# Expert results added into one residual row per token by accumulating indirect DMA, in place of one stored row per token and expert

## The chip, the cores and the metric

The kernel runs on one core of one Trainium2 chip. The metric is the device time of one execution in microseconds (us); three executions of the kernel before took 964.06, 964.85 and 967.42 us, median 964.85. A difference below about 0.3% of it can't be told from no change.

## The reference

Two transformer-like layers over x of 8 batches x 512 tokens x 128 features, each with a mixture of experts:

```
x = layernorm(x + L0_attn(x))        # windowed softmax attention, 16 heads, with its own residual
x = layernorm(x + L0_ffn(x))         # 16 experts of 128 -> 512 -> 128 (gelu), 4 chosen per token
x = layernorm(x + L1_attn(x))        # linear attention with decay, in chunks
x = layernorm(x + L1_ffn(x))         # 8 experts of 128 -> 512 -> 128 (silu gate), 2 chosen per token

L0_ffn:  w = softmax(top-4 logits);  fused = sum_k w[k] * expert[topi[k]](x)
L1_ffn:  w = softmax(top-2 logits);  out   = sum_k w[k] * expert[topi[k]](x) * 12**-0.5
```

The change concerns the two weighted sums over a token's experts, and the addition of x and the layernorm behind each.

## The kernel before

The five engines run programs written out by hand, tied by semaphores; each engine takes its instructions in the order of its program. There are four long stages and a last one.

1. **Attention of layer 0**, batch by batch. Behind it each batch's rows x1 (the output of the first layernorm) are kept in `xres`, the router picks 4 experts per token, and GpSimd scatters each row 4 times into `xs[0]` in DRAM, in which every expert has a region of its own (`scatter`, L651). A row of `xs` holds the row's high and low bf16 halves and one number: the row of `yt` for the result.
2. **Expert tiles of layer 0.** A table made by `tile_table` (L896) lists tiles of 256 rows, each of one expert, expert by expert; it is walked in groups of `RING` = 4 tiles, with two hidden tiles computed ahead. For a tile, SP loads the rows by a transposing DMA (`xt`, L499) and their numbers (`to_now`, L503), TensorE makes the hidden layer (L1715 to L1717) and the output (L1726, L1736), ScalarE does the gelu (L1359) and copies the output from PSUM to `ysb` (`take_out`, L1341), VectorE splits the hidden layer in two bf16 parts (L944, L945), and GpSimd (`store_tiles`, L707) writes `ysb` to `yt` by two indirect DMAs of 128 rows of 512 bytes (L714). Rows of a tile behind the expert's last token have a number out of bounds and are dropped. `yt` has one row for every (token, choice), so no two DMAs touch the same row and none waits for another; ScalarE alone waits for the landing of the tile four before (the ring slot of `ysb`).
3. **Linear attention of layer 1**, `linear_body`, batch by batch, with the sum of layer 0 ahead of it: SP loads the 4 result rows of each token (1 MB per batch, L548, with L558 for the first batch), ScalarE multiplies them by their weights `wres` (`scale_results`, L1388), VectorE adds them and x1 (`pair_up` L971, `add_up` L976; the first batch is done by VectorE alone, L1205), then takes the statistics (`y_stats`) and applies them (`x2_apply`). The other work of a body is the attention, the routing of layer 1 and the scatter to `xs[1]`.
4. **Expert tiles of layer 1**, as stage 2 with three matrices per expert.
5. **The last stage**, for each batch: SP loads the 2 result rows per token (512 KB), VectorE sums with weights (`final_sums`, L1043, 8 operations) and takes the statistics, GpSimd makes the scale and shift (`final_scales`, L697), ScalarE applies them (L1472), SP stores the output (L578). `mv2`, `rstd2`, `minus_mean` and `shift` have one buffer each, `yf` and `ow` two.

The part of `store_tiles` that matters:

```
for u in range(RING):
    pool.wait_ge(to_loaded[n][u], 16 * g + 16)
    pool.wait_ge(y_done[n], RING * g + u + 1)
    for s in range(S2):   # S2 = 2
        pool.indirect_dma_start(out=yt[n][:, :], out_offset=...(to_now[:, u, s:s + 1], 0), in_=ysb[:, u, s, :], ...)
```

Of the kernel before, what the change touches and what calls it, by code (L numbers as in the profile page):

```python
# [52 lines left out]
XW = 2 * D + 2  # L53
# [9 lines left out]
DVE_STEPS_1 = 18  # L63
# [56 lines left out]
def program(nc, x_in, w_all, wq_s, wk_s, wv_t, wo_t, gamma, beta, keys_t, rw_t, rb, b1, b2,  # L120
            w_write, w_read_t, decay, log_alpha, wr, const, const_b, out):
    ctx = ExitStack()
    with ctx:
# [8 lines left out]
        def sem(name):  # L132
# [44 lines left out]
        wres = sb("wres", [P, NT, K0])  # L177
# [32 lines left out]
        table = sb("table", [1, TILES + 1], I32)  # L210

# [45 lines left out]
        to_now = sb("to_now", [P, RING, S2], U32)  # L257
# [9 lines left out]
        gat0 = sb("gat0", [P, 2, T, K0, D])  # L267
# [14 lines left out]
        gat1 = sb("gat1", [P, FIN, T, K1, D])  # L282
        yf = sb("yf", [P, 2, T, D])
        minus_mean = sb("minus_mean", [P, T])
        shift = sb("shift", [P, T])
# [28 lines left out]
        xs = [nc.dram_tensor(f"xs{n}", [experts[n] * REGION, XW], BF16).ap() for n in range(2)]  # L314
        yt = [nc.dram_tensor(f"yt{n}", [B * L * top[n], D], F32).ap() for n in range(2)]
# [8 lines left out]
         ws_ready, decayed, reads_ready, y3_ready, comb_done, out_ready, dlog_ready, x1_spread,  # L324
# [8 lines left out]
                "ws_ready decayed reads_ready y3_ready comb_done out_ready dlog_ready x1_spread "  # L333
                "to_init masks_in logits_taken").split()]

        def pair_of(name):
# [5 lines left out]
         h_ready, act_done, split_done, yp_ready, y_done, tile_step, all_stored, sending) = [  # L342
# [3 lines left out]
                "h_ready act_done split_done yp_ready y_done tile_step all_stored sending").split()]  # L346
# [6 lines left out]
        scaled = sem("scaled")  # L353
        weighted_in = sem("weighted_in")
# [79 lines left out]
        def _(sp):  # L434
# [38 lines left out]
            with sp.Fori(1, CHUNKS_0 // 2) as c:  # L473
                for k in range(2):
                    sp.wait_ge(lo_done, 2 * c + k - 1)
                    sp.dma_start(w_raw[:, k, :], w_all[:, bass.ds((2 * c + k) * CH, CH)]).then_inc(raw_in[k], 16)
            def fill_tails(n):

                sp.wait_ge(tails_ready[n], 1)
                for e in range(experts[n]):  # L480
                    row = sp.value_load(tails[0:1, e:e + 1], min_val=e * REGION, max_val=e * REGION + B * L)
                    sp.dma_start(xs[n][bass.ds(row, TILE), :].rearrange("(p s) d -> p (s d)", s=S2),
                                 tail_rows[:, :, :].rearrange("p s d -> p (s d)")).then_inc(tails_stored[n], 16)
# [4 lines left out]
            def expert_tiles(n):  # L488
# [9 lines left out]
                def load_rows(row, u):  # L498
                    sp.dma_start_transpose(xt[:, u, :, :], xs[n][bass.ds(row, TILE), 0:2 * D]).then_inc(xt_loaded[n][u], 16)  # L499

                def load_numbers(row, u):
                    with nc.allow_non_contiguous_dma(reason="one word of each row"):
                        sp.dma_start(to_now[:, u, :],  # L503
# [79 lines left out]
        def _(pool):  # L583
# [113 lines left out]
            def final_scales(b):  # L697

                pool.wait_ge(var2_ready, 2 * B + b + 1)
                if b:  # L700
                    pool.wait_ge(out_ready, b)
# [1239 lines left out]
```

## Time and profile before

| | us |
|---|---|
| median of three executions | 964.85 |
| lowest, highest | 964.06, 967.42 |
| the profiled execution, first to last instruction (its span; no other time of it is given) | 1145.5 |
| stage 2, first to last store of results | 461.3 to 764.4 |
| stage 3 | 766 to 933 |
| stage 4, first to last store of results | 948.1 to 1100.7 |
| stage 5 | 1101 to 1145.5 |

The profiled execution is 1.187 times as long as the median one: the profile makes the kernel slower, and in which stages it does isn't shown. Times inside it are from its own clock. TensorE is busy for 73% of the span, VectorE for 57%, GpSimd for 46%, ScalarE for 45%. There were 76 tiles in stage 2 (19 groups) and 36 in stage 4 (9 groups).

### The profile page before, as it was taken

What the parts mean: (1) busy time and instruction counts of PE and PEld (TensorE: products, weight loads), DVE (VectorE), ACT (ScalarE), POOL (GpSimd) and SP (SyncE); (2) the same over time, 40 slices, a digit from 0 to 9 for tenths busy, and PEclk for the clock granted to TensorE, in tenths of its full rate; (3) what the DMA queues carried; (4) which work ended last, traced back from release to release, by engine and by line L of the source; (5) the groups of instructions that cost most, each with busy time, mean ns of one, the idle gap of its engine ahead of it and who ended that gap; (6) DMA issues with size and microseconds to landing.
All of it is one profiled execution on the core that took longest, in us unless ns stands there. A gap on an engine that the chain in (4) does not pass through costs nothing.

```text
span 1145.5 us, 35350 instructions
## 1 busy us (share of the span) xinstructions
PE 835.4 (73%) x11802; PEld 642.2 (56%) x11816; DVE 652.7 (57%) x1923; ACT 509.8 (45%) x1290; POOL 525.7 (46%) x538
## 2 busy tenths in 40 slices
PE   4898886877886513887788888847788839999920
PEld 1565555555565401766677667735555529888810
DVE  5457555455544520666565566647787636656656
ACT  2555444444433311544444445426454226656623
POOL 1013634546343471455554555541666644554433
PEclk9899888898857755999898999979887869999965
DMA  6011211112111123433333333323231124222243
GB/s 192 21 31 38 66 34 50 43 44 61 36 48 33 38 74 90 83 68 82 71 79 69 78 86 86 81 85 130 88 122 39 38 84 67 57 55 50 51 131 108
DMA packets 136238, 79.73 MB, mean 70 GB/s; under 512 B 104402, under 2 KB 116857, under 8 KB 136144
## 3 DMA queue, kind: packets, MB, share of 16 engines
q1 hardware_dynamic: 122256, 51.76, 18.7%
q0 software_dynamic: 13312, 25.31, 7.1%
q8 instruction: 67, 1.10, 0.4%
q10 hardware_dynamic: 576, 1.34, 0.4%
q14 instruction: 27, 0.22, 0.1%
HBM read 33.12 MB, written 32.63 MB: 57 GB/s over the span
## 4 chain that ended last, share of the span: by engine, by line
PE 48%; issue 13%; DVE 13%; another core or an unknown queue 9%; ACT 5%; SPq 4%; POOL 4%; DMA 2%; ACTq 1%; DVEq 0%; POOLq 0%
PE avbank L1736 6%; PE proj L1736 5%; PE avbank L1589 4%; PE t L1576 3%; PE t L1717 3%; PE s L1717 3%; PE s L1715 2%; PE t L1715 2%; PE s L1716 2%; PE t L1716 2%; ACT act_out L1359 2%; PE s L1539 2%; POOL xs L655 2%; PE t L1784 2%
## 5 line engine op out<-in xcount | busy, mean ns | idle before, releaser
L714 POOL DMA_INDIRECT yt<-ysb,to_now x224 | 236.8, 1057 | 260.7 <-ACT ysb L1346 197.4
L655 POOL DMA_INDIRECT xs<-x1p,sidx x192 | 189.8, 989 | 196.5 <-ACT prob L1265 111.7
L944 DVE CAST h_hi<-act_out 128x512 bf16<-128x512 f32 x152 | 73.6, 484 | 147.2 <-ACT act_out L1359 113.9
L945 DVE TENSOR_TENSOR h_lo<-act_out,h_hi 128x512 bf16<-128x512 f32 x152 | 107.9, 710 | 5.2
L1265 ACT ACTIVATE prob<-t 128x384 f32<-128x384 f32 (+1 forms) x160 | 74.4, 508 | 78.0 <-PE t L1576 66.1
L1715 PE MATMUL s<-xt,w_hi 128*128 128x256 bf16 x296 | 82.8, 280 | 17.8 <-DMA xt<-xs 13.3
L1736 PE MATMUL avbank<-w_hi,h_hi 128*128 x448 | 89.8, 230 | 7.6 <-issue 6.4
L1736 PE MATMUL avbank<-w_hi,h_lo 128*128 x448 | 87.7, 229 | 3.6 <-issue 3.3
L1736 PE MATMUL avbank<-w_lo,h_hi 128*128 x448 | 87.3, 228 | 2.4 <-issue 2.4
L1736 PE MATMUL proj<-w_hi,h_hi 128*128 x448 | 83.6, 220 | 7.2 <-DVE h_lo L945 5.6
L1717 PE MATMUL t<-xt,w_lo 128*128 128x256 bf16 x296 | 81.5, 275 | 5.9 <-issue 5.9
L1716 PE MATMUL s<-xt,w_hi 128*128 128x256 bf16 x296 | 82.4, 279 | 4.4 <-issue 4.2
L1715 PE MATMUL t<-xt,w_hi 128*128 128x256 bf16 x296 | 81.7, 276 | 4.7 <-issue 4.7
L1717 PE MATMUL s<-xt,w_lo 128*128 128x256 bf16 x296 | 82.2, 278 | 2.6 <-issue 2.6
L1716 PE MATMUL t<-xt,w_hi 128*128 128x256 bf16 x296 | 81.6, 276 | 3.0 <-issue 3.0
L1736 PE MATMUL proj<-w_hi,h_lo 128*128 x448 | 81.2, 219 | 0.5 <-issue 0.5
L1736 PE MATMUL proj<-w_lo,h_hi 128*128 x448 | 81.1, 218 | 0.5 <-issue 0.5
L1359 ACT ACTIVATE act_out<-t,b_sb 128x256 f32<-128x256 f32 x152 | 61.4, 480 | 44.1 <-remote 36.8
L824 DVE RECIPROCAL rden<-avbank 128x96 f32<-128x96 f32 (+1 forms) x40 | 31.8, 796 | 82.9 <-PE avbank L1589 66.3
L1791 PE MATMUL proj<-cb 128*128 128x512 bf16 x164 | 44.0, 416 | 42.1 <-DMA xs<-x1p,sidx 26.2
L1589 PE MATMUL avbank<-prob,one_of 128*32 128x96 f32 (+1 forms) x1280 | 70.7, 287 | 3.0 <-issue 3.0
L1589 PE MATMUL avbank<-prob,vf 128*32 128x96 f32 (+1 forms) x1280 | 68.6, 291 | 2.0 <-issue 1.2
(235 smaller groups left out, 2131.4 us busy)
## 6 DMA issues: line engine op xcount, KB each, us to landing
w_raw<-w_all SPq DMA_DIRECT2D x59, 256.0 KB
gat<-yt SPq DMA_DIRECT2D x7, 1024.0 KB, 5.3
gat<-yt SPq DMA_DIRECT2D x10, 512.0 KB, 4.5
yt<-ysb,to_now POOLq DMA_INDIRECT x224
xs<-tail_rows SPq DMA_DIRECT2D x24, 129.0 KB
xs<-x1p,sidx POOLq DMA_INDIRECT x192
out<-ow SPq DMA_DIRECT2D x8, 256.0 KB, 2.3
xt<-xs SPq DMA_TRANSPOSE x112
```

Of the source, the lines that this page charges most:

```text
L655: pool.indirect_dma_start(out=xs[n][:, :], out_offset=bass.IndirectOffsetOnAxis(sidx[:, par, at:at + 1], 0), in_=x1p[:, par, t, k, :], in_ ...
L714: pool.indirect_dma_start(out=yt[n][:, :], out_offset=bass.IndirectOffsetOnAxis(to_now[:, u, s:s + 1], 0), in_=ysb[:, u, s, :], in_offset= ...
L944: ch.link(dve.tensor_copy(h_hi[:, par, c, :], act_out[:, par, c, :]))
L945: dve.tensor_tensor(h_lo[:, par, c, :], act_out[:, par, c, :], h_hi[:, par, c, :], ALU.subtract).then_inc(split_done[n], 1)
L1265: nc.scalar.activation(prob[:, g, 0:width], t_bank[g % 2][:, 0:width], ACT.Exp, scale=SCALE).then_inc(exp_done, 1)
L1359: ins = nc.scalar.activation(act_out[:, par, c, :], h_bank[2 * par + c // 2][:, (c % 2) * TILE:(c % 2 + 1) * TILE], ACT.Gelu, bias=b1_sb[: ...
L1589: ins = pe.matmul(dst[32 * t:32 * t + 32, 0:nq], value_block(par, w, t, g) if dst is num_ps else ones, prob[:, g, t * nq:(t + 1) * nq], st ...
L1715: pe.matmul(dst, w_h, xt[:, u, 0, :], start=True, stop=False)
L1716: pe.matmul(dst, w_h, xt[:, u, 1, :], start=False, stop=False)
L1717: return pe.matmul(dst, w_l, xt[:, u, 0, :], start=False, stop=True)
L1736: ins = pe.matmul(dst, x[:, par, c, rows], w, start=(n == 1 and c == 0 and m == 0 and k == 0), stop=True, skip_group_check=True)
L1791: pe.matmul(proj[1][:, :], ident_b, band4, start=True, stop=True)
```

## The change

Each layer gets one DRAM tensor `acc` with one row per token (and 256 spare rows). It is filled with x1 by a plain DMA (`fill_sums`); then each tile's output, already multiplied by the token's weight on ScalarE, is *added* to the token's row by the indirect DMA (`compute_op=ALU.add`). What is loaded afterwards is the finished sum x + sum of w*y, 256 KB per batch in both layers. `scale_results`, `pair_up`, `add_up`, the sums of the first batch and `final_sums` are gone.

Since an addition reads the row and writes it later, two that touch one row must not overlap. Tiles of one expert have different tokens; tiles of different experts may share tokens. So a scatter waits for the landing of the tile before it where the expert changes (a flag, `new_of`, made by `tile_table`, is the number added to a semaphore count), and for the landing of the tile two before always. The first two groups (8 tiles) wait for the tile before each time. A row of `xs` carries two words now, the number and the weight; `to_now` is read by ScalarE before it takes the output out. Padding rows have weight 0 and are added to spare rows. In layer 0 the rows of `acc` are in the order in which a partition's four tokens lie together, and the output of the kernel is stored 2 KB per partition in place of 512 bytes.

The last stage has `mvf`, `rstdf`, `minus_mean` and `shift` in two buffers, and works on `gat1` directly.

```
+            def fill_sums(n, b):
+                rows = acc[n][bass.ds(b * L, L), :]
+                rows = rows.rearrange("(p t) d -> p t d", p=P) if n == 0 else rows.rearrange("(t p) d -> p t d", p=P)
+                sp.wait_ge(x1_kept, B * n + b + 1)
+                apart(sp)
+                sp.dma_start(rows, xres[:, bass.ds(b * T, T), :]).then_inc(acc_filled[n], 16)
...
                 if b + 2 < B:
-                    sp.wait_ge(comb_done, b + 1)
+                    sp.wait_ge(x2_ready, b + 1)
                     load_outputs(0, b + 2)
+                if b:
+                    fill_sums(1, b - 1)
...
             def store_tiles(n):
                 def group(g):
+                    new = None
+                    if not (type(g) is int and g < 2):
+                        _, new = nc.values_load_multi_w_load_instructions(
+                            new_of[0:1, bass.ds(RING * g, RING)], engines=(mybir.EngineType.Pool,), min_val=0,
+                            max_val=16 * S2)
                     for u in range(RING):
-                        pool.wait_ge(to_loaded[n][u], 16 * g + 16)
                         pool.wait_ge(y_done[n], RING * g + u + 1)
-                        pool.sem_inc(sending[n], 1)
+                        before, last = (u - 1) % RING, (u - 2) % RING
+                        if type(g) is int and g < 2:
+                            if u > 0 or g > 0:
+                                pool.wait_ge(y_stored[n][before], 16 * S2 * (g + 1 if u else g))
+                        else:
+                            pool.wait_ge(y_stored[n][before], 16 * S2 * (g if u else g - 1) + new[u])
+                            pool.wait_ge(y_stored[n][last], 16 * S2 * (g + 1 if u > 1 else g))
+                        pool.sem_inc(sending, 1)
                         for s in range(S2):
                             pool.indirect_dma_start(
-                                out=yt[n][:, :], out_offset=bass.IndirectOffsetOnAxis(to_now[:, u, s:s + 1], 0),
-                                in_=ysb[:, u, s, :], in_offset=None, bounds_check=B * L * top[n] - 1,
-                                oob_is_err=False).then_inc(y_stored[n][u], 16)
+                                out=acc[n][:, :], out_offset=bass.IndirectOffsetOnAxis(to_now[:, u, s, 0:1], 0),
+                                in_=ysb[:, u, s, :], in_offset=None, compute_op=ALU.add).then_inc(y_stored[n][u], 16)
...
                 def take_out(j, u, use):
-                    act.wait_ge(yp_ready[n], j + 1)
                     if not (type(use) is int and use == 0):
                         act.wait_ge(y_stored[n][u], 16 * S2 * use)
-                    nc.scalar.copy(ysb[:, u, :, :], y_bank[u % 2][:, 0:S2 * D].rearrange("p (s d) -> p s d", s=S2)
-                                   ).then_inc(y_done[n], 1)
+                    act.wait_ge(to_loaded[n][u], 16 * use + 16)
+                    act.wait_ge(yp_ready[n], j + 1)
+                    for s in range(S2):
+                        ins = nc.scalar.activation(ysb[:, u, s, :], y_bank[u % 2][:, s * D:(s + 1) * D], ACT.Identity,
+                                                   scale=to_now[:, u, s, 1:2].bitcast(F32))
+                    ins.then_inc(y_done[n], 1)
...
-            def final_sums(b):
+            def final_stats(b):
                 par = b % 2
...
+                dve.wait_ge(gathered[1][b % FIN], 16 * (b // FIN) + 16)
+                if b > 1:
+                    dve.wait_ge(scaled, b - 1)
+                stats(lambda t: gat1[:, b % FIN, t, :], statf, mvf[:, par, :, :], vef[:, par, :], var2_ready)
...
                 if nxt:
-                    x2_apply(b + 1)
-                if nxt2:
-                    pair_up(b + 2, par)
-                    add_up(b + 2, par)
+                    x2_apply(b + 1, 1 - par)
                 take_logits(1, b)
...
-            dve.tensor_copy(table[0:1, TILES:TILES + 1], xbank[0:1, 2 * P:2 * P + 1]).then_inc(table_kept[n], 1)
+            dve.tensor_scalar(new_of[0:1, :], xbank[0:1, 2 * P:2 * P + TILES], float(16 * S2), None, ALU.mult)
+            dve.tensor_copy(table[0:1, TILES:TILES + 1], xbank[0:1, 3 * P:3 * P + 1]).then_inc(table_kept[n], 1)
```

**GpSimd's loop over the groups of expert tiles of layer 0** (the body of `store_tiles`, its first two tiles), before: two stores per tile behind the tile's numbers (`to_loaded`) and its output (`y_done`).

```order
L394 UNCONDITIONAL_BRANCH
L394 ISA
L711 ISA [waits to_loaded0_0]
L714 DMA yt<-ysb,to_now 16384x128 [waits y_done0]
L714 DMA yt<-ysb,to_now 16384x128
L711 REGISTER_ALU [waits to_loaded0_1]
L714 DMA yt<-ysb,to_now 16384x128 [waits y_done0]
L714 DMA yt<-ysb,to_now 16384x128
```

The same place now:

```order
L398 UNCONDITIONAL_BRANCH
L398 ISA
L733 TENSOR_LOAD new_of
L733 ISA x8
L737 REGISTER_ALU
L743 ISA [waits y_done0]
L744 REGISTER_ALU [waits y_stored0_3]
L747 DMA acc<-ysb,to_now 4352x128 [waits y_stored0_2]
L747 DMA acc<-ysb,to_now 4352x128
L737 REGISTER_ALU
L743 REGISTER_ALU [waits y_done0]
L747 DMA acc<-ysb,to_now 4352x128 [waits y_stored0_0,y_stored0_3]
```

Each group begins with a load of four flags into registers, and each tile's first DMA waits for the two ring slots before its own.

**VectorE in a body of the linear attention**, from the application of the last statistics to the logits, before (`gat` are loaded results, `y` the sum, `lg` the logits of layer 1):

```order
L987 TENSOR_SCALAR x2w<-y,mv,rstd 128x128 [waits rstd2_ready]
L987 TENSOR_SCALAR x2w<-y,mv,rstd 128x128 x3
L969 SCALAR_TENSOR_TENSOR gat<-gat 128x4x256 [waits weighted_in]
L99 REGISTER_ALU
L969 SCALAR_TENSOR_TENSOR y<-gat,xres 128x512 [waits dve_step]
L99 REGISTER_ALU
L969 SCALAR_TENSOR_TENSOR y<-gat,y 128x512 [waits dve_step]
L833 COPY lg<-xbank 128x4x8 [waits lg_ready1,comb_done]
```

and now:

```order
L1052 TENSOR_SCALAR x1f<-y,mv,rstd 128x128 [waits x1_kept,rstd3_ready]
L1052 TENSOR_SCALAR x1f<-y,mv,rstd 128x128 x3
L1017 TENSOR_SCALAR x2w<-gat,mv,rstd 128x128 [waits rstd2_ready]
L1017 TENSOR_SCALAR x2w<-gat,mv,rstd 128x128 x3
L867 COPY lg<-xbank 128x4x8 [waits lg_ready1]
```

The three additions between `x2w` and the logits are gone, so VectorE stands at the wait for the logits (`lg_ready1`) that much earlier.

## Rows read from the trace of the kernel before

**Rows 1.** The page: the span, and the chain that ended last, by engine.

```profile
span 1145.5 us, 35350 instructions
...
PE 48%; issue 13%; DVE 13%; another core or an unknown queue 9%; ACT 5%; SPq 4%; POOL 4%; DMA 2%; ACTq 1%; DVEq 0%; POOLq 0%
```

**Rows 2.** Stages 2, 3, 4: length; busy PE, PEld, DVE, ACT, POOL; clock; DMA.

```profile
461.00:765.00 304.00, 246.27 (x2829) 207.61 (x2827) 182.78 (x316) 147.63 (x389) 159.16 (x152) 0.95 0.33 74
766.00:933.00 167.00, 118.01 (x607) 78.94 (x618) 119.85 (x544) 71.35 (x203) 92.15 (x90) 0.81 0.29 93
948.00:1100.00 152.00, 139.13 (x1645) 125.56 (x1642) 93.70 (x204) 93.85 (x238) 77.00 (x72) 1.00 0.27 54
```

**Rows 3.** GpSimd's timeline, stage 2: start, length, what, [idle before, releaser].

```profile
574.95 0.97 POOL L714 DMA_INDIRECT yt<-ysb,to_now  x1 [2.26 <-ACT ysb L1346]
576.23 1.15 POOL L714 DMA_INDIRECT yt<-ysb,to_now  x1 [0.30 <-issue]
```

**Rows 4.** Timeline of GpSimd, end of stage 2.

```profile
763.46 0.98 POOL L714 DMA_INDIRECT yt<-ysb,to_now  x1 [0.30 <-issue]
765.87 0.10 POOL L740 MEMSET x_t<- 128x1 f32 x1 [1.43 <-DMA yt<-ysb,to_now]
```

**Rows 5.** Timeline of ScalarE in stage 2, where a group begins.

```profile
568.99 0.37 ACT L1346 COPY ysb<-proj 128x256 f32<-128x256 f32 x1 [4.09 <-remote]
569.26 1.57 ACT L1359 ACTIVATE act_out<-t,b_sb 128x256 f32<-128x256 f32 x4
```

**Rows 6.** Waits of TensorE within stage 2: total us, times, longest.

```profile
PE avbank L1726 <- ACT ysb L1346: 7.9, 9, 1.1
```

**Rows 7.** Timeline of SP's queue in stage 2: eight table values are loaded between these.

```profile
564.85 0.02 SPq L523 DMA_DIRECT2D w_raw<-w_all  x1
568.82 0.38 SPq L503 DMA_DIRECT2D to_now<-xs  x1
```

**Rows 8.** Timeline of VectorE and ScalarE, start of stage 3.

```profile
769.65 0.61 DVE L1205 SCALAR_TENSOR_TENSOR y<-gat,wres,xres 128x128 f32<-128x128 f32 x2 [10.16 <-DMA gat<-yt]
...
774.73 0.87 DVE L772 BATCH_NORM_STATS2 stat<-y 128x6 f32<-128x128 f32 x4
...
783.04 1.15 DVE L996 TENSOR_TENSOR pm<-t,decay_m 128x512 f32<-128x512 f32 x2
...
774.05 4.79 ACT L1393 ACTIVATE gat<-gat,wres 128x128 f32<-128x128 f32 x16 [12.73 <-DMA gat<-yt]
```

**Rows 9.** Timeline of one body of stage 3, several engines.

```profile
845.16 1.21 DVE L969 SCALAR_TENSOR_TENSOR gat<-gat 128x1024 f32<-128x1024 f32 x1
...
847.99 0.19 DVE L833 COPY lg<-xbank 128x32 f32<-128x32 f32 x1
...
856.08 0.68 DVE L1009 SCALAR_TENSOR_TENSOR y<-x2w,proj 128x512 f32<-128x512 f32 x1
...
846.00 1.07 PE L1679 MATMUL xbank<-wr_sb,x_tl 128*128 128x8 f32 x8
...
852.76 2.49 PE L1804 MATMUL proj<-vv,pm 128*128 128x128 f32 x20
```

**Rows 10.** Timeline of stage 5: VectorE, GpSimd, ScalarE; and the landing of the output stores.

```profile
1106.13 1.14 DVE L1052 SCALAR_TENSOR_TENSOR yf<-gat,wres,xres 128x128 f32<-128x128 f32 x4 [12.18 <-DMA gat<-yt]
...
1108.47 0.87 DVE L772 BATCH_NORM_STATS2 stat<-yf 128x6 f32<-128x128 f32 x4
...
1109.94 1.13 DVE L1052 SCALAR_TENSOR_TENSOR yf<-gat,wres,xres 128x128 f32<-128x128 f32 x4
...
1110.13 0.25 POOL L702 TENSOR_SCALAR minus_mean<-mv 128x4 f32<-128x4 f32 x1 [9.46 <-DVE ve L778]
...
1111.53 0.25 POOL L705 TENSOR_TENSOR shift<-minus_mean,rstd 128x4 f32<-128x4 f32 x1
...
1111.82 1.65 ACT L1472 ACTIVATE ow<-yf,shift,rstd 128x128 f32<-128x128 f32 x4 [16.19 <-POOL shift L705]
...
DMA to landing us min/median/max: 2.3/2.3/2.8
```

More of the change, by code:

```diff
@@ L52 @@
 CPB_0 = CHUNKS_0 // B
-XW = 2 * D + 2
+XW = 2 * D + 4
+NUM, WT = slice(2 * D, 2 * D + 2), slice(2 * D + 2, XW)
 RING = 4
@@ L476, in _ @@
                     sp.dma_start(w_raw[:, k, :], w_all[:, bass.ds((2 * c + k) * CH, CH)]).then_inc(raw_in[k], 16)
+            def fill_sums(n, b):
[4 more added lines that the diff above has]
+                sp.dma_start(rows, xres[:, bass.ds(b * T, T), :]).then_inc(acc_filled[n], 16)
+            for c in range(1, CPB_0):
+                load_chunks(c)
+            with sp.Fori(2, B) as b:
+                for c in range(CPB_0 // 2):
+                    load_chunks(CPB_0 // 2 * b + c)
+                fill_sums(0, b - 2)
+            for b in range(B - 2, B):
+                fill_sums(0, b)
             def fill_tails(n):
@@ L498, in load_rows @@
                 def load_rows(row, u):
-                    sp.dma_start_transpose(xt[:, u, :, :], xs[n][bass.ds(row, TILE), 0:2 * D]).then_inc(xt_loaded[n][u], 16)
+                    sp.dma_start_transpose(xt[:, u, :, :], xs[n][bass.ds(row, TILE), 0:D].bitcast(BF16)).then_inc(xt_loaded[n][u], 16)
                 def load_numbers(row, u):
-                    with nc.allow_non_contiguous_dma(reason="one word of each row"):
-                        sp.dma_start(to_now[:, u, :],
-                                     xs[n][bass.ds(row, TILE), 2 * D:XW].bitcast(U32).rearrange(
-                                         "(s p) o -> p (s o)", s=S2)).then_inc(to_loaded[n][u], 16)
+                    with nc.allow_non_contiguous_dma(reason="two words of each row"):
+                        sp.dma_start(to_now[:, u, :, :],
+                                     xs[n][bass.ds(row, TILE), D:XW // 2].rearrange(
+                                         "(s p) o -> p s o", s=S2)).then_inc(to_loaded[n][u], 16)
                 def numbers_of(row, u, tile, use):
@@ L719, in store_tiles @@
                 pool.wait_ge(table_kept[n], 1)
-                more = over_tiles(pool, n, group)
+                pool.wait_ge(acc_filled[n], 16 * B)
+                apart(pool)
+                more = over_tiles(pool, n, group, head=2)
                 for u in range(RING):
@@ L1220, in _ @@
             expert_tiles(1)
-            dve.wait_ge(x1_kept, 2 * B)
             for b in range(B):
-                final_sums(b)
+                final_stats(b)
         @block.scalar
```

182 lines of the change are left out of this document (67 added, 115 removed).

## The prediction

> **What bounds the kernel now.** I read the page first: the chain that ended last is TensorE for 48%, waits named "issue" for 13% and VectorE for 13% of the span, GpSimd for only 4% [rows 1]. Then the windows by stage, since the change acts differently in each [rows 2]. The reader is to see there that stage 4 is TensorE's (139 of 152 us), that stage 2 is nobody's (the busiest, TensorE, 246 of 304), and that stage 3 has VectorE busy for 120 of 167 us beside a TensorE at clock 0.81. Attention is touched only by DMAs on SP and one word more per row, and I cost it at nothing: the fills wait there for `x1_kept` of two batches before, which lies behind by the time SP has issued a batch's weight loads.
>
> Then GpSimd's own timeline in stage 2. One indirect DMA takes 0.97 to 1.15 us and the next starts 0.30 later; GpSimd then waits 2.26 us for ScalarE [rows 3]. So a tile costs GpSimd about 2 x 1.28 = 2.56 us, of a tile's 304/76 = 4.0 us: a group of four needs 10.3 of 16.0. From the last DMA's end to what waits for its landing are 1.43 us [rows 4]. ScalarE's copy of the output stands 0.37 us long ahead of the gelu of the next tile [rows 5], and TensorE waits for that copy 9 times in the stage, 7.9 us in total [rows 6].
>
> **What goes, part by part.**
>
> *Between stages 2 and 3.* The sums of the first batch run from 769.65 to 774.73 [rows 8]: 5.1 us between the load and the statistics, all on the path. They go. The load is a quarter of the size, but here the first half of it already released the sums, so I take nothing for it. The sums of the second batch keep VectorE until the decays begin at 783.04 [rows 8]; without them the decays begin when TensorE's scores are there, which I put at 0.7 us of gain. Together 5.8 us.
>
> *In stage 3*, six bodies lose the additions, from 845.16 to 847.99, 2.8 us of VectorE each [rows 9]. They don't all come back, since the next thing, the logits, ends on TensorE at 846.00 + 1.07 = 847.07 [rows 9]: 0.9 us gained there. Then the scores, the values and the reads on TensorE end at 852.76 + 2.49 = 855.25, and VectorE takes them at 856.08 [rows 9]: 0.8 us gained. ScalarE's 16 multiplications, 4.79 us [rows 8], go too, but ScalarE idles in a body anyway. I take 0.8 x 6 = 5 us; the bounds are 0.6 x 6 = 4 and, if all of the additions came back, 2.8 x 6 = 17. The loads and fills stand on SP ahead of a weight chunk that is wanted a body later; hidden, and worth under a microsecond each if not.
>
> *In stage 5* a batch comes every 1109.94 - 1106.13 = 3.81 us, VectorE being the bound. Of that 1108.47 - 1106.13 = 2.34 are the sums [rows 10]. What is left is 1.47 on VectorE; 1.65 on GpSimd (1110.13 to 1111.78) and 1.65 on ScalarE [rows 10], which now have two buffers. Next comes the store: `ow` has two buffers, so two batches take at least 1.65 of ScalarE, 0.4 of issue and 2.3 to landing [rows 10], 2.2 us a batch. With some contention I take 2.3. The gain is 2.34 for the first batch and 7 x (3.81 - 2.3) = 10.6 for the rest, 12.9 us. Bounds: 9 and 16.
>
> The savings are 5.8 + 5 + 12.9 = 23.7 us.
>
> **What comes.**
>
> *The output through a multiplication.* ScalarE's 16 activations of 128x128 take 4.79 us, 0.30 each [rows 8], so the two of a tile take 0.60 in place of 0.37 [rows 5]: 0.23 us more. Stage 4 hides it behind TensorE. In stage 2 it delays TensorE in the 9 places where it waits for the copy [rows 6] and delays the gelu behind it wherever ScalarE is late, which is once or more per group [rows 5]. I take 30 tiles, 7 us; the bounds are 9 x 0.23 = 2 and 112 x 0.23 = 26. ScalarE waits for the tile's number and weight too, which SP loads about 5 us ahead.
>
> *The fixed waits.* Working through the reference's routing for its drawn inputs, layer 0 has 73 tiles with rows and 3 empty ones (flagged, as my reading of the table gives), layer 1 has 36. Behind the first eight tiles, 13 tiles begin an expert in layer 0 (16 with the empty ones) and 7 in layer 1, about one in each group. How late an accumulating DMA lands no row shows. It can't be earlier than the plain one, 1.43 us [rows 4]; above it lies a read from DRAM, and a whole load until its data is used took 769.65 - 765.87 = 3.8 [rows 4, 8], which makes 5.2 at most. I take 2.1, near the lower end, since the plain landing of 256 KB in DRAM is 2.3 [rows 10]. By the Trainium skill ("DMA: Bandwidth & Descriptors", the anatomy of one SWDGE DMA) a DMA issued by GpSimd has a fixed cost of some 2.0 us, most of it the write's receipt; by that figure the landing would be 2.0 even without a read in front, and the stage ends below would cost 1 us more.
>
> At the end of stage 2 the three empty tiles are stored one behind the other, each 1.4 us or so later than now: 4 us. At the end of stage 4, 1 us.
>
> *GpSimd within the stages.* Four flags are loaded per group. SP loads eight values in at most 568.82 - 564.87 = 3.95 us [rows 7], so four take 2. One ordered tile per group waits 2.1 + 0.2. GpSimd then needs 10.3 + 2 + 2.3 = 14.6 us a group, in place of 10.3. In the profiled execution a group has 16.0, so this fits, and the ring of four slots takes up what is uneven. In the median execution, if the 180 us that the profile adds lay evenly, a group has 16.0 / 1.187 = 13.5. If GpSimd's own times don't shrink, it is short by 1.1 us in 17 groups, 19 us; if they shrink alike, by nothing. I take 4 us. Stage 4 is TensorE's: 9 groups of 16.9 us, nothing.
>
> The cost of one accumulating DMA to GpSimd isn't in the trace either. The lower bound is the plain one's, 0.98; the upper is twice it, if GpSimd writes a read of the row beside each read of the source. I take 0.98, since the rows, their count and the numbers are the same, and keep the other end for the range.
>
> The costs are 7 + 5 + 4 = 16 us. **The sum**: -23.7 + 16 = -8 us: 1137.5 in place of a span of 1145.5. The profiled span is 181 us above the median run. The terms are lengths of single instructions and landings, so I subtract them unscaled: 964.85 - 8 = 957 us.
>
> **The rivals.**
>
> A, the forecast, 948 to 962 us, likeliest at 957.
>
> B, *stages 3 and 5 give back everything*: TensorE's fillers and GpSimd's order in stage 3 shift with VectorE, so the bodies gain nearly 2.8 us. For it: VectorE is the busiest there [rows 2]. Against: TensorE's logits and reads end within 0.9 us of VectorE's use [rows 9]. That is 12 us more, 945.
>
> C, *slower: GpSimd becomes the bound of stage 2.* The place is its queue of ordered scatters; what decides is whether a group's need, 14.6 us, passes a group's time. In the profile that takes 0.18 us more per DMA, or a landing 1.4 us later; in a faster run nearly nothing. The ring then fills, ScalarE waits for `y_stored` and TensorE for ScalarE. With 1.2 us per DMA the need is 16.4; against a group between 13.5 and 16.0 it is short by 0.4 to 2.9, 7 to 49 us in 17 groups, mean 28. The time is 957 - 4 + 28, and with some in stage 4, 985. For it: nobody is far ahead in stage 2, and the additions read before they write. Against: GpSimd waited 2 to 2.6 us twice a group [rows 3]. A rule of the Trainium skill (same page, latency facts) puts an HBM access at 0.2 us on average and 2 us under high load; at the high figure the landing would be 3.4 us and C would hold in both layers, at the low one A. No row tells which load this is.
>
> D, *the copies eat it*: all 76 tiles of stage 2 pay the 0.23 us, 17 in place of 7: 967, about what it was. For it: ScalarE's late copies [rows 5]. Against: it is half idle [rows 2].
>
> That the change doesn't do what it says, with each tile waiting for the one before, would need 36 and 13 more waits that hurt only as C does; it is counted there.
>
> **How the numbers follow.** Chances: A 0.42, B 0.11, C 0.38, D 0.09. About 0.3% (962 to 968) can't be told from no change. Faster: 0.37 of A and B make 0.48. The same: 0.05 of A and most of D, 0.12. Slower: C and the rest, 0.40. The predicted time is A's, 957. The range takes in B down to 942 and C up to 1002, its price with a group of 13.5; beyond lies a DMA of twice the cost or a landing of 5 us. A's own range is 948 to 962.
>
> **What would show it.** Right: in stage 5 a batch every 2.1 to 2.5 us; about 5 us less between the last landing of stage 2 and the first reads; a body of stage 3 shorter by 0.5 to 1 us; accumulating DMAs under 1.1 us on GpSimd, idle before most of them for ScalarE, and stage 2 within 10 us of 304. C would show as GpSimd waiting for its own DMAs, ScalarE's output waiting for `acc`, and groups of over 16 us. The prediction is wrong if an accumulating DMA costs GpSimd over 1.2 us or lands later than 3 us, or if the savings of stage 5 drown in DMA traffic.

## The result and the profile after

The changed kernel takes 1097.2 us (median of 4 runs, 1096.0 to 1097.9), the kernel before 966.1 (4 runs, three of them those given ahead, 964.1 to 967.8): a ratio of 1.1375 [1.134, 1.141]. The forecast was 957 us and the range ended at 1002; the time is 95 us beyond it, in the direction of rival C and at over five times its price.

The profile of before shown above had a span of 1145.5 us. Profiled once more, the same kernel has a span of 967.0, and every stage length of before in what follows is from that second profile. The sentence ahead of the prediction that the profile makes the kernel slower doesn't hold with it: this profiled execution took 968.8 us. It begins so, first before, then after (the page's span, engines and GpSimd's queue):

```profile
span 967.0 us, 35350 instructions
PE 754.3 (78%) x11802; PEld 600.3 (62%) x11816; DVE 652.8 (68%) x1923; ACT 519.3 (54%) x1290; POOL 522.6 (54%) x538
q0 software_dynamic: 13312, 25.31, 8.2%
```

```profile
span 1095.9 us, 35384 instructions
...
q0 software_dynamic: 38400, 27.49, 18.1%
...
L747 POOL DMA_INDIRECT acc<-ysb,to_now x224 | 364.5, 1627 | 183.7 <-issue 78.1
```

GpSimd's indirect DMAs mark the stages. The table takes, from GpSimd's timeline, the start of the first and of the last one of each stage, in us:

| stretch | before | after | difference |
|---|---|---|---|
| start to first output store | 373.2 | 370.1 | -3.1 |
| stage 2, 152 stores (19 groups) | 219.4 | 347.2 | +127.8 |
| between stages 2 and 3 | 40.4 | 33.7 | -6.7 |
| stage 3 (64 scatters) | 130.1 | 131.7 | +1.6 |
| between stages 3 and 4 | 16.5 | 15.5 | -1.1 |
| stage 4, 72 stores (9 groups) | 141.7 | 170.0 | +28.3 |
| last store to the end | 45.8 | 27.7 | -18.1 |

So the time lies in the two expert stages, and the savings came in sum nearly as priced. The windows of stages 2 and 4, before and then after (columns: window, length, busy us and count of each engine, TensorE's clock, DMA share, GB/s), show who filled them:

```profile
373.00:593.00 220.00, 211.92 (x2817) 194.41 (x2813) 170.80 (x316) 150.70 (x387) 161.76 (x152) 1.00 0.47 103
780.00:921.00 141.00, 136.45 (x1640) 125.28 (x1638) 100.89 (x203) 99.57 (x237) 69.39 (x71) 1.00 0.28 58
```

```profile
370.00:717.00 347.00, 261.15 (x2824) 220.58 (x2821) 176.38 (x316) 166.06 (x464) 246.75 (x151) 0.90 0.53 70
898.00:1068.00 170.00, 140.76 (x1644) 126.08 (x1641) 94.98 (x204) 102.63 (x273) 114.64 (x71) 0.97 0.44 51
```

In stage 2 before, TensorE is busy for 212 of 220 us at the full clock: the stage is TensorE's. GpSimd is close behind: 161.8 us in 152 DMAs, and the 0.30 us between two of them 152 times, is 207 of 219. After, GpSimd has 246.8 in 151 DMAs, 1.63 each. Its timeline has 23 gaps of 2.4 to 3.2 us, one ahead of every tile that has to wait for the one before, together 61.5 us, and 128 gaps of 0.30. That is all of the 347 us. The view of the waits names fewer of them, since it puts six of the 23 to "issue":

```profile
ACT ysb L1349 <- DMA to_now<-xs: 101.6, 45, 4.7
...
POOL acc L747 <- DMA acc<-ysb,to_now: 49.1, 26, 3.2
```

(waits of stage 2 after: waiting engine and line, releaser, total us, times, longest.) The first row is ScalarE's: it waits for the numbers of a slot that SP reloads only once GpSimd's stores of four tiles ago have landed. That is GpSimd's lateness seen from ScalarE. The view of the store's line, before and after:

```profile
L714 POOL DMA_INDIRECT yt<-ysb,to_now x224: 977/984/1362, 373.2 to 921.2; - x112
...
DMA to landing us min/median/max: 2.1/2.3/3.1
```

```profile
L747 POOL DMA_INDIRECT acc<-ysb,to_now x224: 1552/1554/2071, 370.1 to 1068.2; - x112
...
DMA to landing us min/median/max: 3.2/3.4/5.2
```

An adding DMA occupies GpSimd for 1.55 us where a plain one takes 0.98 (medians), and lands 3.4 us after its start, 1.1 later than a plain one. GpSimd's timeline at the start of stage 2, after, where each of the first eight tiles waits for the one before:

```profile
376.27 1.61 POOL L747 DMA_INDIRECT acc<-ysb,to_now  x1 [2.65 <-DMA acc<-ysb,to_now]
378.18 1.58 POOL L747 DMA_INDIRECT acc<-ysb,to_now  x1 [0.30 <-issue]
382.53 1.55 POOL L747 DMA_INDIRECT acc<-ysb,to_now  x1 [2.76 <-issue]
...
394.94 1.56 POOL L747 DMA_INDIRECT acc<-ysb,to_now  x1 [2.44 <-issue]
```

And in the middle of stage 2, after, where both patterns stand:

```profile
558.63 1.55 POOL L747 DMA_INDIRECT acc<-ysb,to_now  x1 [0.30 <-issue]
560.48 1.55 POOL L747 DMA_INDIRECT acc<-ysb,to_now  x1 [0.30 <-issue]
565.11 1.57 POOL L747 DMA_INDIRECT acc<-ysb,to_now  x1 [3.07 <-DMA acc<-ysb,to_now]
566.98 1.55 POOL L747 DMA_INDIRECT acc<-ysb,to_now  x1 [0.30 <-ACT ysb L1349]
568.84 2.07 POOL L747 DMA_INDIRECT acc<-ysb,to_now  x1 [0.30 <-issue]
571.22 1.55 POOL L747 DMA_INDIRECT acc<-ysb,to_now  x1 [0.30 <-issue]
575.42 1.55 POOL L747 DMA_INDIRECT acc<-ysb,to_now  x1 [2.65 <-DMA acc<-ysb,to_now]
```

Two or more adding DMAs back to back, 0.30 apart; then a flagged tile waits for the one before. In [rows 3] GpSimd waited 2.26 us for ScalarE; in the second profile of before it is 1.0 us once in eight DMAs, so most of the room that I saw there wasn't the kernel's.

In stage 5 VectorE, after, keeps only the statistics, which answers to [rows 10]:

```profile
1084.47 0.87 DVE L806 BATCH_NORM_STATS2 statf<-gat 128x6 f32<-128x128 f32 x4 [0.45 <-DMA gat<-acc]
...
1086.30 0.87 DVE L806 BATCH_NORM_STATS2 statf<-gat 128x6 f32<-128x128 f32 x4 [0.27 <-DMA gat<-acc]
...
1088.45 0.87 DVE L806 BATCH_NORM_STATS2 statf<-gat 128x6 f32<-128x128 f32 x4 [0.59 <-DMA gat<-acc]
```

A batch comes every 2.0 us in place of 3.81, and VectorE waits for the loads.

### The profile page after: what moved, and what is told of

Its sections match the earlier page's. It is cut to its first block and busy times, and to the rows that moved or that the text cites. A ratio compares the mean times of both kernels' runs of the same rounds, so it can differ in the third digit from the quotient of the medians.

```text
span 1095.9 us, 35384 instructions
## 1 busy us (share of the span) xinstructions
PE 807.3 (74%) x11804; PEld 627.4 (57%) x11818; DVE 615.0 (56%) x1826; ACT 505.3 (46%) x1291; POOL 648.5 (59%) x540
## 3 DMA queue, kind: packets, MB, share of 16 engines
q0 software_dynamic: 38400, 27.49, 18.1%
## 5 line engine op out<-in xcount | busy, mean ns | idle before, releaser
L747 POOL DMA_INDIRECT acc<-ysb,to_now x224 | 364.5, 1627 | 183.7 <-issue 78.1
L982 DVE CAST h_hi<-act_out 128x512 bf16<-128x512 f32 x152 | 69.9, 460 | 178.5 <-ACT act_out L1363 176.6
L1721 PE MATMUL avbank<-w_hi,h_hi 128*128 x448 | 94.0, 233 | 41.8 <-DVE h_lo L983 36.3
L1700 PE MATMUL s<-xt,w_hi 128*128 128x256 bf16 x296 | 86.4, 292 | 13.6 <-DVE hid L993 13.3
L1349 ACT ACTIVATE ysb<-avbank,to_now 128x128 f32<-128x128 f32 x112 | 35.0, 363 | 122.3 <-DMA to_now<-xs 81.9
L1701 PE MATMUL s<-xt,w_hi 128*128 128x256 bf16 x296 | 85.9, 290 | 0.0
L1702 PE MATMUL s<-xt,w_lo 128*128 128x256 bf16 x296 | 85.5, 289 | 0.0
L1700 PE MATMUL t<-xt,w_hi 128*128 128x256 bf16 x296 | 83.2, 281 | 0.0
L1701 PE MATMUL t<-xt,w_hi 128*128 128x256 bf16 x296 | 83.1, 281 | 0.0
L1721 PEld LDWEIGHTS avbank<-w_hi,h_hi 128*128 128x128 bf16 x448 | 45.8, 102 | 54.7 <-issue 51.9
L1349 ACT ACTIVATE ysb<-proj,to_now 128x128 f32<-128x128 f32 x112 | 35.1, 364 | 88.8 <-DMA to_now<-xs 63.1
L993 DVE TENSOR_TENSOR hid<-act_out,s 128x256 f32<-128x256 f32 x72 | 28.0, 419 | 69.2 <-ACT act_out L1373 69.0
```

What stands on the lines that cost most here:

```text
L747: pool.indirect_dma_start(out=acc[n][:, :], out_offset=bass.IndirectOffsetOnAxis(to_now[:, u, s, 0:1], 0), in_=ysb[:, u, s, :], in_offset= ...
L982: ch.link(dve.tensor_copy(h_hi[:, par, c, :], act_out[:, par, c, :]))
L993: dve.tensor_tensor(hid[:, par, c, :], act_out[:, par, c, :], h_bank[c][:, TILE:2 * TILE], ALU.mult).then_inc(gated, 1)
L1349: ins = nc.scalar.activation(ysb[:, u, s, :], y_bank[u % 2][:, s * D:(s + 1) * D], ACT.Identity, scale=to_now[:, u, s, 1:2].bitcast(F32))
L1700: pe.matmul(dst, w_h, xt[:, u, 0, :], start=True, stop=False)
L1701: pe.matmul(dst, w_h, xt[:, u, 1, :], start=False, stop=False)
```

## The experiments

Three theories stood at the start. T1: the adding DMA's own price on GpSimd, 0.57 us more for each of 224. T2: the ordering waits and the late landing. T3: ScalarE's multiplication with its wait for number and weight. The times are medians; stage lengths are measured as in the table above.

**The kernel before, again.** 

> The kernel before, unchanged, profiled anew, to have stage lengths of an execution whose span is near its time. If the first profile's 180 extra microseconds lay mostly ahead of stage 2 (it began at 461 us there and at 370 in the changed kernel), the span is near 965, stage 2 is near 300 us and stage 4 near 150. If they lay evenly, stage 2 is near 304 / 1.187 = 256 us and stage 4 near 128.

Measured: 968.8 us, span 967.0. Stage 2 is 219.4 us, stage 4 141.7. The first profile had 302.2 between the same two stores of stage 2 and 151.6 in stage 4, and 88 us more ahead of stage 2. Its waits have rows, over the whole run, of which the second profile has none (98 us of the first two lie in stage 2, 35 us of such rows in stage 4, where TensorE hides most of it):

```profile
ACT ysb L1346 <- remote: 79.8, 43, 4.1
...
ACT act_out L1359 <- remote: 43.8, 18, 4.6
ACT mov L1260 <- remote: 34.0, 10, 5.0
```

The first expectation had it wrong too: of the extra 180 us, 83 lay within stage 2. A group of four tiles really takes 219.4 / 19 = 11.5 us, not the 16.0 or 13.5 of the prediction. What "remote" waited for, no run shows.

**Plain stores in the changed kernel (e1).** A token's row keeps only its last result.

```diff
-  in_=ysb[:, u, s, :], in_offset=None, compute_op=ALU.add)
+  in_=ysb[:, u, s, :], in_offset=None)
```

> The changed kernel with its indirect DMAs writing in place of adding; every wait, flag and number stays. A token's row then holds its last result alone, so the sums are not made. Theory 1 (an adding DMA costs GpSimd 1.55 us or more in place of 0.98, and GpSimd's queue of 8 DMAs a tile group sets the pace): the DMAs go back to about 1.0 us, a group of four costs GpSimd 8 x 0.6 = 4.8 us less, and the 28 groups 134 us at most: 970 to 1000 us. Theory 2 (the ordering waits and the late landing set the pace, whatever the DMA's own cost): over 1060 us, with GpSimd idle in front of the flagged tiles as before. Theory 3 (ScalarE's multiplication and its wait for number and weight): 1090 or more, nothing changes.

Measured: 973.8 and 991.6 us in two runs; the profile is of the slower one, so its lengths may hold some 18 us too much, and stage 2 begins 4 to 7 us late in it. Of the 131 us that the changed kernel is over before, 123 go with the adding alone by the faster run (106 by the slower).

```profile
L747 POOL DMA_INDIRECT acc<-ysb,to_now x224: 953/962/1482, 377.3 to 960.4; - x112
its engine sat idle before it (us, times) until:
  DMA acc<-ysb,to_now: 91.7, 60
```

The ordering waits are all there, 91.7 us under that name. The kernel is 8 us over before by the faster run (26 by the slower) although two stretches save 26 (9.3 between the stages 2 and 3, 16.4 at the end), so ordering costs 33 us (at most 51), ScalarE's two multiplications included. Stage 2 has 262.8 us; stage 4 has 142.3, no more than before, since the waits fit into GpSimd's room there: all its gaps sum to 71.5 us, and to 72.0 before. T3 falls here; with plain DMAs, T2 holds for stage 2 alone and for the smaller part.

**Adding without ordering (e2).** The kernel before with `compute_op=ALU.add` in its stores, each to a row of its own, and SP filling these rows in stage 1 and 3.

> The kernel before, with its stores to a row of its own for each token and choice made adding ones; the rows are filled ahead with x1 by SP, so that the sums hold x1 once more per choice (the output is another one). No flags and no ordering waits. With the two plain kernels and the changed one this makes a table of two by two: adding or not, ordered or not. Theory 1 (the price of an adding DMA to GpSimd, 1.55 us, is its own, whatever the rows it adds to and whatever waits stand around it): 1.55 us each as in the changed kernel, a group costs GpSimd 8 x (1.55 + 0.30) = 14.8 us against 11.5 before; stage 2 goes from 219 to about 285 us, stage 4 stays TensorE's (9 x 14.8 = 133 against 142): 1025 to 1040 us in all. Theory 2 (ordering and landing are the cost, or the price comes from rows that several DMAs add to): the DMAs come out near 1.0 us and the time within 15 us of the kernel before.

Measured: 1058.0 us, ratio 1.095 [1.089, 1.101]; stage 2 292.3 us. The expectation was 18 us low, for two reasons: stage 2 came out 7 longer, since the mean DMA is 1.61 and not 1.55, and the other values of x2 route layer 1 into ten groups of tiles in place of nine (80 stores, 160.1 us; a group takes 16.0 as against 15.7).

```profile
L727 POOL DMA_INDIRECT yt<-ysb,to_now x232: 1552/1555/2071, 371.7 to 1009.2; - x116
its engine sat idle before it (us, times) until:
  issue: 68.9, 198
```

The price is the adding kind's, with distinct rows and no waits too. 152 DMAs at 1.62 (its window of stage 2 has GpSimd busy for 246.8 us) and 0.30 make 292.4, the measured 292.3: GpSimd alone is the stage. The four kernels make a table (us; a stage from its first store to its last, its first two groups to the first store of the third; in these each tile waits where the kernel is ordered):

| stretch | plain | ordered (e1, at most) | adding (e2) | both |
|---|---|---|---|---|
| stage 2 | 219.4 | 262.8 | 292.3 | 347.2 |
| its first two groups | 22.9 | 38.7 | 31.0 | 46.1 |
| stage 4 | 141.7 | 142.3 | 160.1 (ten groups) | 170.0 |
| its first two groups | 32.5 | 37.1 | 32.9 | 47.7 |

In stage 2 adding costs 73 and 84, ordering 43 and 55. The two ordered kernels also have ScalarE's two multiplications, which the others lack and which cost 8.8 by e3 where nothing hides them, so the 43 is not all ordering. In stage 4 neither alone costs much (0.6 us ordered, 0.3 a group adding), and both cost 28.3: adding takes up the room into which the waits fitted.

**ScalarE's part alone (e3).** The kernel before with two activations by a scale of one in place of the copy, behind a wait for the tile's numbers.

> The kernel before, with ScalarE's copy of each output replaced by two multiplications (by one), and with the changed kernel's wait for the tile's numbers ahead of them; the stores to a row of their own for each choice, and all sums, stay. Theory 3 (this is what costs the time): 1030 us or more. Theory 1: 967 to 992, that is 2 to 26 us more than before, the bounds that the prediction gave; its value was 7.

Measured: 972.5 us, ratio 1.008 [1.005, 1.011], 7.2 us more than before; the prediction's term was 7. The two activations take 2 x 0.36 us, not 2 x 0.30, in place of 0.37. Stage 2 has 228.2 us (+8.8), stage 4 141.7 (0). T3 is settled: as large as forecast, and no cause of 131 us.

**Every tile flagged (e4).**

> The changed kernel with the flag set in every tile, so each tile's scatter waits for the one before to land: about 52 more waits in layer 0 and 21 in layer 1, 73 in all. If GpSimd's queue is the path in both layers, each costs what a flagged tile waits now, 2.3 to 2.9 us: 73 x 2.5 = 180 us more, 1280 us. If the queue has room, and the time is lost elsewhere, 1097 to 1130 us.

Measured: 1254.7 us, 157.5 more than the changed kernel: 2.2 us for each of 73 added waits. Stage 2 has 457.7 us (+110.5), stage 4 216.7 (+46.7), where every microsecond now counts since GpSimd has no room left.

```profile
L747 POOL DMA_INDIRECT acc<-ysb,to_now x224: 1552/1553/2077, 374.5 to 1225.4; - x112
its engine sat idle before it (us, times) until:
  DMA acc<-ysb,to_now: 247.0, 94
```

It also shows that the flag does what it says. By GpSimd's gaps of over 1.2 us the changed kernel waits 37 times: seven times in the first two groups of each stage, then 16 times in stage 2 and seven in stage 4, which are the numbers that the prediction read out of the routing. This one waits 110 times, 73 more. (The view's 94 misses the waits that it calls "issue", and counts some gaps of 0.30.)

**What the adding DMA's price hangs on (e5, e6).** Half of the rows (`ysb[0:P // 2, u, s, :]` and as many numbers), then half of the columns (`ysb[:, u, s, 0:D // 2]` into rows of 64).

> The changed kernel with half of each adding store: 64 rows of 512 bytes per DMA, the other rows are not added. It tells what an adding DMA's price hangs on. Packets were 144 per adding DMA and 32 per plain one (worked out from queue 0's counts). If the price follows the rows and their packets, the DMA falls from 1.55 to about 1.2 us or less on GpSimd and stage 2 from 347 by some 50 us; if it is a fixed price of the adding kind, it stays at 1.5.

> The changed kernel with 64 of the 128 columns added: 128 rows of 256 bytes per DMA (the other half of each output is not added, and the rows land at other places). If the price follows the number of rows: 1.55 us as before and 1090 to 1100 us. If it follows the bytes: as with half of the rows.

Measured, in this order, 1066.6 and 1091.4 us:

```profile
L747 POOL DMA_INDIRECT acc<-ysb,to_now x224: 1392/1408/1926, 373.0 to 1035.1; - x112
```

```profile
L747 POOL DMA_INDIRECT acc<-ysb,to_now x224: 1552/1554/2074, 374.6 to 1061.6; - x112
```

Half of the bytes changes nothing (1.554 us); half of the rows takes 0.146 us off, 2.3 ns a row. Neither expectation for e5 was right: the price follows the rows only in its smaller part, 0.29 of 1.55 us if that slope holds down to no rows, and 1.26 us would be fixed. Stage 2 went from 347.2 to 326.9, 20 us and not 50. The packets of GpSimd's queue are 24064 here. With 192 scatters of 32 packets in each kernel (13312 in 416 plain DMAs are 32 each), an adding DMA of 128 rows has (38400 - 6144) / 224 = 144, one of 64 rows 80. So packets follow the rows, one each and 16 more; GpSimd's time mostly doesn't. What the fixed part is, no run shows.

**Stage 3: the additions cut (e7).** `pair_up` and `add_up` of the kernel before on one column of 128, in the bodies only.

> The kernel before with the additions in the bodies of stage 3 cut to one column of 128 (the sums of the batches from the third on are not made; ScalarE's multiplications, all waits and the first two batches stay). My prediction's step for stage 3: 0.8 us gained in each of six bodies, the period falls from 17.9 to 17.1 us. The rival that the traces suggest (a body is TensorE's chain of turns, logits, scores, values and reads, whose length follows its granted clock: 17.2 us at 0.90, 18.0 at 0.81, 19.0 at 0.73, with the additions or without): the period stays within 0.3 us of what its clock gives, and VectorE waits 2 us or more for the logits in place of adding.

Measured: 962.1 us in one run. The additions stand in the first six of the eight bodies. The periods between VectorE's y3 (a `y<-x2w,proj` in its timeline) that hold them are 15.0, 18.2, 18.1, 17.8, 17.0 and 16.9 us here, mean 17.2; in the kernel before 16.0, 18.1, 18.1, 17.4, 18.2 and 17.9, mean 17.6; in the changed kernel 14.9, 18.9, 18.2, 19.0, 17.5 and 18.0, mean 17.8. (The 17.9 of the expectation is a mean that leaves out the first of these and takes in the last body, which has no additions.) The windows of three bodies each, first of the kernel before, then of this one (the clock is third from the end):

```profile
618.10:634.10 16.00, 13.18 (x80) 8.76 (x81) 13.95 (x65) 11.27 (x32) 3.74 (x3) 1.00 0.22 67
652.20:670.30 18.10, 15.51 (x77) 10.54 (x78) 14.38 (x66) 10.76 (x30) 11.59 (x12) 0.81 0.32 102
670.30:687.60 17.30, 13.97 (x77) 9.23 (x78) 13.97 (x65) 9.30 (x30) 11.85 (x12) 0.90 0.34 107
```

```profile
615.60:630.50 14.90, 13.20 (x82) 8.72 (x81) 11.77 (x64) 11.12 (x32) 3.22 (x3) 1.00 0.23 75
630.50:648.70 18.20, 14.45 (x73) 10.02 (x72) 12.46 (x65) 8.10 (x25) 11.40 (x12) 0.81 0.35 104
684.60:701.60 17.00, 13.81 (x78) 9.08 (x77) 12.35 (x66) 9.05 (x28) 11.03 (x12) 0.90 0.16 47
```

Bodies at a clock of 0.81 take 17.8 to 18.2 us here and 17.9 to 18.2 in the kernel before; at 0.90 they take 16.9 to 17.0 here and 17.4 there; the first, at 1.00, takes 15.0 here and 16.0 there. So the additions are worth nothing at 0.81, 0.4 us at 0.90 and 1.0 at 1.00: the rival's expectation holds for the first, the prediction's step of 0.8 about for the last. (The clock of a window is a mean over stretches at 1.2 and at 2.4 GHz; the four turns of x1f take 1.12 us in the one and 0.66 in the other.) VectorE waits for the logits instead of adding (the changed kernel, in a body):

```profile
794.60 1.36 DVE L1017 TENSOR_SCALAR x2w<-gat,mv,rstd 128x128 f32<-128x128 f32 x4
798.68 0.19 DVE L867 COPY lg<-xbank 128x32 f32<-128x32 f32 x1 [2.72 <-PE xbank L1664]
```

**Stage 3: more fillers in the changed kernel (e9).** `keep_busy(16)` to `keep_busy(25)`.

> The changed kernel with 25 filler matmuls in place of 16 in each body of stage 3, nothing else. If the step for stage 3 failed only because TensorE's chain ran at a lower granted clock, the clock goes to 0.9 or 1.0 here, and the bodies, which have no additions, fall below the 17.1 us that the same fillers gave with additions: to about 16.5, and the whole from 1097 to about 1087. If what is left is fixed by something else, they come out at 17.1 or more and the whole at 1091.

Measured: 1091.1 us in one run. The fillers reach into TensorE's wait for x1f, 2.5 us before and 1.6 now. The mean period from the second body on falls from 18.2 to 16.9 us, between the two expectations, at clocks that alternate:

```profile
779.00:796.00 17.00, 14.61 (x91) 9.60 (x90) 11.87 (x61) 4.42 (x12) 11.48 (x12) 1.00 0.28 82
796.00:813.00 17.00, 16.43 (x79) 10.89 (x81) 12.16 (x61) 5.47 (x12) 10.44 (x12) 0.80 0.26 74
```

The bodies of this kernel take 15.7 to 15.9 us at 1.00 and 18.2 at 0.81, so the clock is worth 2.4 us of a body. It isn't all: h3 below has the same fillers, and its bodies with the additions take 17.1 to 17.4 us at 1.00. Those two kernels differ in more than the additions, but with the first body of e7 it says that work taken off VectorE comes back at the full clock and not at the lower one.

**Keeping what is worth it (h1, h2, h3).** h1: plain stores, no flags, weights in the rows for both layers, unweighted adds, doubled small tiles in stage 5. h2: the same in layer 1 alone. h3: h2 with 25 fillers in a body of stage 3. Their core, in `final_sums` and in the stores' source:

```diff
-   ins = dve.scalar_tensor_tensor(out=yf[:, par, t, :], in0=gat1[:, b % FIN, t, k, :],
-                                  scalar=wres[:, b * T + t, k:k + 1], in1=before, ...
+   ch.link(add(yf[:, par, :, :], gat1[:, b % FIN, :, 0, :], xres[:, b * T:b * T + T, :]))
+   add(yf[:, par, :, :], gat1[:, b % FIN, :, 1, :], yf[:, par, :, :]).then_inc(comb_done, 1)
```

> From the kernel before: what seemed good of the change without its adding stores. The weights travel in the rows to the experts and ScalarE multiplies each output by them, in both layers; the stores stay plain, each to a row of its own; VectorE sums unweighted in adds of 128x512, and the last stage's small tiles are doubled. Terms: stage 5 a batch every 1.47 + 2 x 0.69 = 2.9 us in place of 3.8, 7 to 9 us gained; between the stages 2 and 3 about 1; ScalarE's multiplications cost what the third experiment measured, about 7. That is 960 to 967 us. If the copies' cost was layer 0's alone, this is where it shows: stage 2 about 8 us longer than before, stage 4 as before.

> The same in layer 1 alone, where TensorE hides ScalarE's second activation; layer 0 is as in the kernel before. Expected: stage 2 to 4 as before, stage 5 about 37 us in place of 45.8: 955 to 960 us, 0.5 to 1% under the kernel before. If stage 5 is bound by something besides VectorE's sums (the loads of 512 KB or the stores), 962 to 966.

> The kernel with weights in the rows for layer 1 alone, and 25 filler matmuls in place of 16 in each body of stage 3: TensorE waited 2.5 us for x1f behind them, and nine more at 0.23 us fill 2.1 of that. If the body's length follows the granted clock and the clock follows TensorE's idle time, it rises towards 0.9 or more, the bodies fall from 17.7 to 17.2 us or less, and the whole gains 3 to 6 us: 955 to 958. If the clock doesn't rise, the time stays at 961 (or 2 us over it, if the fillers run into the turn).

Measured: h1 964.8 us, ratio 0.998 [0.996, 1.001], no change that can be told. h2 961.3, 0.995 [0.992, 0.998]. h3 957.1, 0.991 [0.989, 0.993]: 9 us under the kernel before and 140 under the changed one. h1 loses 5 us in stage 2 (224.4) that h2 doesn't (219.6). The last stretch gained 2.8 us and not 8 (43.0 in h2): VectorE's two adds took 0.69 each as priced, but it then waits for a buffer in every other batch, so a batch comes every 3.65 us. h3's timeline:

```profile
924.64 0.17 DVE L787 TENSOR_SCALAR vef<-mvf 128x4 f32<-128x4 f32 x1
926.19 0.69 DVE L982 SCALAR_TENSOR_TENSOR yf<-gat,xres 128x512 f32<-128x512 f32 x1 [1.37 <-ACT ow L1486]
```

h3's bodies run at a clock of 0.90 to 1.00, h2's at 0.81 to 0.90; from the second one on they take 17.1 us in the mean, h2's 17.6, with the same additions.

## Why the prediction was wrong

By its own steps:

1. **The length of a group: wrong, and it made up a room that wasn't there.** "In the profiled execution a group has 16.0 ... in the median execution 13.5". It was 11.5. The one profile shown was 181 us above the timed runs, I knew it, and I spread the difference evenly. Of it, 83 us sat in stage 2, beside waits that name no work of the kernel ("remote"). e1, the changed kernel without the adding, took 974 us, 17 over the forecast and inside the range: that is all that this step and the others but step 4 make together.
2. **"Stage 2 is nobody's": wrong with it.** It is TensorE's, 212 of 220 us, with GpSimd at 207 of 219. The room was 12 us in the stage, not 6 us in each group.
3. **GpSimd's need, "10.3 + 2 + 2.3 = 14.6": right but for the flags.** The mean plain DMA is 1.06 us and not 0.98, so the 10.3 was 10.9; the flags' 2 us don't show, since a group that begins with no wait begins after the usual 0.30. That leaves 13.2, and the 17 groups behind the first two take 13.2 each in e1. By my own terms, 14.6 against 11.5 is rival C with certainty, 53 us in 17 groups, before any dearer DMA.
4. **"I take 0.98": wrong, 0.57 us too low on the median, and the step that put the time beyond the range.** 1.55 lies inside the bounds that I had written (0.98 to twice it), but the range took in only 1.2. With 1.63 + 0.30 a group needs 15.4 us for its stores alone, more than a group had. Against e1 it is worth 123 us of the whole (106 by the slower run): 84 in stage 2, and in stage 4, where I had put nothing, the 28 that it costs together with the ordering.
5. **The first two groups: put at nothing without a reason.** The sum prices the 17 groups behind them, but each of the first eight tiles waits for the one before. With adding DMAs these seven waits cost 15 us in stage 2 (46.1 against 31.0 in e2), and the first two groups of stage 4 take 15 us more than before (47.7 against 32.5), over half of what that stage lost.
6. **The landing, 2.1 us: about right.** From the end of the last store to what waits for it are 1.9 us at the end of stage 2 after; an ordered tile waits 2.4 to 3.2, where I had 2.3. What makes up the rest no row says. The Trainium skill gives some 2.0 us as the fixed cost of a DMA issued by GpSimd, setup and completion together ("DMA: Bandwidth & Descriptors", the anatomy of one SWDGE DMA). From the start of the instruction to the landing the plain store has 2.3 us, near it, and the adding one 3.4, well above. (That by the 2.0 the stage ends would cost 1 us more doesn't follow in the prediction: it is under the 2.1 that was taken.)
7. **The 7 us for ScalarE's multiplication: right in size, in part by luck.** It is 7.2 by e3, 8.8 of it in stage 2 with 2 given back behind it; but my 0.23 us a tile was 0.35, so fewer than the 30 tiles can have paid it in full. Rival D is settled with it.
8. **Between stages 2 and 3, -5.8 with 4 back: the gain was 6.7**, since the late landing costs 0.5 at the end of the stage (1.9 against 1.4) and not 4; the empty tiles' waits lie ahead of the last store and count in stage 2.
9. **Stage 3, -5: wrong, +1.6.** The additions ran beside TensorE's chain of turns, logits, scores and reads, and most of what VectorE saved went into its wait for the logits. e7 puts their worth at nothing to 0.4 us in the bodies at 0.81 and 0.90, and at 1.0 only in the first, which runs at the full clock; I had 0.8 in each of six. The changed kernel has two bodies at a clock of 0.73, of 18.9 and 19.0 us (before: 0.81 to 0.90 behind the first), which took back more than the first body gained, and e9 shows the body shorter once the clock is up. Why the clock fell to 0.73 in these two stays open.
10. **Stage 5, -12.9: right in kind, too small**, a batch every 2.0 us (I took 2.3), 18.1 us in all with the smaller loads, over my bound of 16.

Outside the two expert stages the change saved 27 us (3.1 + 6.7 - 1.6 + 1.1 + 18.1), against 23.7 forecast, near it only because stage 5 gave 5 more and stage 3 some 7 less. What failed is the cost side of one engine's queue: C was the right mechanism, at 156 us in place of 28.

The prediction weighed the latency facts of the same page of the Trainium skill, 0.2 us on average and 2 us under high load for an HBM access, the latter for C. From the end of a DMA to its landing the medians are 2.3 - 0.98 = 1.3 us plain and 3.4 - 1.55 = 1.9 adding: 0.5 us more. If that is the read, it is nearer to the low figure; no run parts it from the rest of the landing. C held all the same, since it hung on the group's length and on the DMA's price on GpSimd.

## What to carry to other kernels

Before an engine's room is priced, the profile's span has to agree with the timed runs; where it doesn't, profile again and look for wait kinds that are no work of the kernel, and take the engine's busy time against the timed length, not against the profiled one. Moving sums into GpSimd's adding DMAs moves VectorE work of which most was hidden onto a serial queue at 1.9 us per 128 rows, and 2.4 us or more for each wait between dependent ones: count that queue first, the special first rounds of its loop with it, against the shortest length its stage can have. A stage with room for either cost, as stage 4 here, can lack it for both. Where a price lies between bounds a factor of two apart, and the near end alone fits the room, the bound that doesn't fit belongs in the range.

## What was not expected of the hardware

An indirect DMA that adds has 144 packets for 128 rows where a plain one has 32, and takes GpSimd 1.55 us in place of 0.98 whether the row is 512 or 256 bytes, and 1.41 with half of the rows. TensorE's granted clock moves a body of stage 3 more than VectorE's load does. With 9 filler matmuls more in a body it was 0.90 to 1.00 in h3 (0.81 to 0.90 in h2), while in e9 some bodies rose to 1.00 and others stayed at 0.81. And GpSimd's power of 128x4 takes 1.56 us when it starts beside VectorE's adds of 128x512, but 1.04 while VectorE waits (the two rows, in this order, stage 5 of h3) and 1.04 beside VectorE's statistics too (stage 5 of the changed kernel):

```profile
929.86 1.56 POOL L712 TENSOR_TENSOR rstdf<-vef,cf 128x4 f32<-128x4 f32 x1
...
932.40 1.04 POOL L712 TENSOR_TENSOR rstdf<-vef,cf 128x4 f32<-128x4 f32 x1
```
